# One block for three phases, K and V products sharing half of the array, and new orders of issue in a two-layer attention kernel

## The reference

```
x = x + L0_xattn(layernorm(x), ctx)   # 16 heads of 16, q from x, k and v from ctx (192 channels)
x = x + L0_ffn(layernorm(x))          # switch: 8 experts, 256 -> 1024 -> 256, 512 rows each
x = x + L1_xattn(layernorm(x), ctx)   # 16 heads of 16 with biases, then relu(. @ W1) @ W2
x = x + L1_ffn(layernorm(x))          # six nodes, each an attention of 8 heads of 32
```

## Time and profile before

| what | us |
|---|---|
| median of three runs | 4030.45 |
| profiled execution, its own time | 4034.15 |
| profiled execution, span from first to last instruction | 4032.1 |
| TensorE busy in the span | 3956.1 |
| VectorE, ScalarE, GpSimd busy | 2384.4, 2656.5, 1852.6 |
| first layer, experts, second layer end about | 624, 862, 4032 |
| from issue to landing, median: a store of an expert's rows from ScalarE's queue | 2.2 |
| from the start of `f.x2:0` (870.85) to the end of `f.rs:0` | 3.0 |

### The profile page before, as it was taken

The page is one execution under the profiler, slowest core; times in us unless marked ns, Lnnn a source line. Parts: engine busy times, 40 slices in busy tenths (PEclk is TensorE's granted clock), DMA queues, the critical chain, the costliest instruction groups (busy, mean ns, idle before and its releaser), DMA issues.

```text
span 4032.1 us, 100880 instructions
## 1 busy us (share of the span) xinstructions
PE 3956.1 (98%) x38276; PEld 3369.6 (84%) x38276; DVE 2384.4 (59%) x6216; ACT 2656.5 (66%) x11851; POOL 1852.6 (46%) x1979
## 2 busy tenths in 40 slices
...
GB/s 103 74 106 76 67 58 147 166 81 25 15 12 15 17 14 14 14 14 14 14 13 13 14 13 21 12 12 12 13 12 12 12 12 12 13 13 12 4 4 9
DMA packets 117868, 129.74 MB, mean 32 GB/s; under 512 B 12007, under 2 KB 110677, under 8 KB 117265
## 3 DMA queue, kind: packets, MB, share of 16 engines
...
...
## 4 chain that ended last, share of the span: by engine, by line
PE 76%; DVE 1%; ACT 1%; POOL 0%; issue 0%; DMA 0%; POOLq 0%; DVEq 0%
PE c_product L1552 35%; PE c_product L1563 14%; PE c_product L1614 11%; PE c_scores L1604 7%; PE c_product L1637 5%; PE c_product L1625 2%; PE c_product L1653 1%; PE c_product L1664 1%; DVE c_qT L1407 1%; PE c_product L1540 1%; PE c_product L1662 1%; ACT c_front_probs L1364 0%; ACT c_probs L1364 0%; PE c_product L1691 0%; DVE c_neg_max L1416 0%
## 5 line engine op out<-in xcount | busy, mean ns | idle before, releaser
L1318 POOL TENSOR_TENSOR c_probs<-c_probs,c_row_inv 128x512 f32<-128x512 f32 x744 | 766.5, 1042 | 1436.6 <-DVE c_row_inv L1419 1432.9
L1364 ACT ACTIVATE c_probs<-c_scores,c_neg_max 128x128 f32<-128x128 f32 x2976 | 1054.9, 398 | 432.7 <-DVE c_neg_max L1416 432.4
L1552 PE MATMUL c_product<-c_nodes,cell_w 128*128 128x256 f32 x4352 | 1049.7, 382 | 1.5 <-DVE c_nodes L1478 0.8
L1552 PEld LDWEIGHTS c_product<-c_nodes,cell_w 128*128 128x128 f32 x4352 | 794.8, 190 | 108.8 <-issue 7.3
L1416 DVE TENSOR_REDUCE c_neg_max<-c_scores 128x4 f32<-128x512 f32 x1024 | 664.7, 676 | 104.9 <-PE c_scores L1604 98.9
L1364 ACT ACTIVATION_READ_ACCUMULATOR c_probs<-c_scores,c_neg_max 128x1 f32 x2976 | 703.5, 236 | 0.0
L1370 ACT COPY c_probsT<-c_product 128x512 f32<-128x512 f32 x744 | 416.6, 616 | 235.9 <-PE c_product L1614 229.4
L1364 ACT ACTIVATE c_front_probs<-c_scores,c_neg_max 128x128 f32<-128x128 f32 x1120 | 404.6, 406 | 176.6 <-DVE c_neg_max L1416 176.4
L1563 PE MATMUL c_product<-cell_w,c_nodes 128*128 128x256 f32 x1792 | 435.3, 383 | 0.5 <-DVE c_x L1469 0.5
L474 ACT ACTIVATE a_probs<-a_scores,a_neg_max 128x128 f32<-128x128 f32 x1024 | 360.4, 410 | 47.9 <-DVE a_neg_max L545 47.6
L1614 PE MATMUL c_product<-consts_sb,c_probs 128*128 128x128 f32 x2976 | 385.8, 273 | 0.1
(11 more groups left out here) (185 smaller groups left out, 6457.8 us busy)
## 6 DMA issues: line engine op xcount, KB each, us to landing
...
```

The source lines that it names most:

```text
L1318: nc.gpsimd.tensor_tensor(e, e, rinv[:, i, r].unsqueeze(2).broadcast_to([P, 4, T]), ALU.mult).then_inc(norm_made, 1)
L1364: a = nc.scalar.activation(probs(n, j)[:, r, k], S[r][:, k], ACT.Exp, bias=nmax[:, i, r, k:k + 1], accum_out=rsum[:, i, r, k:k + 1])
L1552: i = T_.matmul(m[:, u], w[:, k, u * P:(u + 1) * P], src[:, k], start=n == 0, stop=n == last)
```

## The change

1. One `nc.Block()` is opened in `build` for all three phases. Semaphores live in a frame around it. The meeting of all engines between phases is replaced by waits: SyncE and TensorE of the experts wait until all products of the first layer are read; VectorE waits until its stores have landed; GpSimd of the second layer waits until the experts' rows have landed; TensorE's third bank of the second layer waits for VectorE's last read of the experts.
2. In the first layer a `K` that is followed directly by `V` of the job before takes the half-step form of the second layer. With the new tables that is so for job 3 and jobs 5 to 29, 26 of 32.
3. All tables of the first layer are new (repeated step, head, tail), and ScalarE gets a tail of its own there.
4. Heads and tails of the second layer are new; its repeated steps are not changed.

```
 FIRST_PE_ORDER = """
-Tn:6 Q:1 T0.1:3 T1.1:3 S0:1 A:3 r.n:7 K:0 O:3 T1.0:2 T0.0:2 S1:1 L:6 Tx:0 V:1
+K:2 V:3 Q:2 L:8 T0.1:4 T1.1:4 S0:2 A:4 Tn:7 Tx:1 r.n:8 O:4 T1.0:3 T0.0:3 S1:2
 FIRST_DVE_ORDER = """
-O^:3 S1.i3:2 st1:3 S0.i1:1 S0.i3:1 S0.i0:1 S0.i2:1 S1.x3:1 S1.x2:1 S1.x1:1 Tx^:0 L^:6 S1.x0:1 r.sh:6 V^:1
-Tn^:5 Q^:0 r.oh:6 S1.i1:1 S1.i0:1 st:-1 S0.x2:0 S0.x0:0 S0.x3:0 A^:2 r.n^:6 S1.i2:1 S0.x1:0 mk:-2 K^:-1
+S0.x3:4 S1.i2:5 A^:6 Tn^:9 r.n^:10 Tx^:3 S0.x0:4 O^:6 S0.i3:5 st1:6 S1.x1:4 S1.x3:4 S1.x0:4 S1.x2:4 S1.i1:4
+K^:3 V^:4 Q^:3 L^:9 r.sh:9 S1.i0:4 st:2 S0.i1:4 S1.i3:4 mk:2 r.oh:9 S0.i0:4 S0.i2:4 S0.x2:3 S0.x1:3
 FIRST_ACT_ORDER = """
-nm:-1 T0^1:1 S1.e3:0 S1.e2:0 S1.e1:0 r.ex:5 S1.e0:0 T0^3:1 T0^2:1 T1^3:1 T1^2:1 S0.e2:-1 S0.e3:-1 S0.e0:-1
-S0.e1:-1 T1^0:0 T1^1:0 T0^0:0
+S0.e0:4 T1^0:5 T1^1:5 T0^0:5 T0^1:5 S1.e1:4 S1.e0:4 S1.e2:4 S1.e3:4 T0^3:5 r.ex:9 T0^2:5 T1^2:5 T1^3:5 nm:2
+S0.e2:3 S0.e1:3 S0.e3:3
 FIRST_POOL_ORDER = """
-S0.n3:2 nm1:4 put:11 S0.n1:2 S1.n0:2 rs:0 S0.n2:2 S1.n1:2 S0.n0:2 S1.n2:2 S1.n3:2 rs1:3
+S0.n2:3 S0.n0:3 S1.n2:3 S0.n3:3 rs1:4 nm1:4 put:11 S1.n0:2 rs:0 S1.n1:2 S1.n3:2 S0.n1:2
...
+                    if after != ("V", j - 1):
+                        project(product(n, j), wk, ct[:, o]).then_inc(prod, 1)
+                    else:
+                        keys_m = product(n, j)
+                        for u in range(2):
+                            T_.matmul(keys_m[:, u], wk[:, 0, u * P:(u + 1) * P], ct[:, o, 0], start=u == 0, stop=False)
...
+                        for b in range(PAIR):
+                            T_.matmul(m[:, b], ct[:, o, 0, b * T:(b + 1) * T], wv[:, 0], start=b == 0, stop=False)
+                        for u in range(2):
+                            k = T_.matmul(keys_m[:, u], wk[half[0], 1, u * P:(u + 1) * P], ct[half[0], 1 - o, 1], start=False, stop=u == 1)
+                            v = T_.matmul(m[:, u], ct[half[1], o, 1, u * T:(u + 1) * T], wv[half[1], 1], start=False, stop=u == 1)
...
-        block = es.enter_context(nc.Block())
...
+            sp.wait_ge(*first["emptied"])
...
+            pe.wait_ge(*first["emptied"])
...
+            for s, n in first["stored"]:
+                dve.wait_ge(s, n)
...
+            for s, n in early["rows_of_experts"]:
+                pool.wait_ge(s, n)
...
+                elif i == BANKS // 2:
+                    pe.wait_ge(*early["experts_emptied"])
...
 PE_HEAD = """
-F6:0 F7:0 B6:0 B7:0 F8:0 f.Tx:0 f.K:0 f.V:0 f.Q:0 F9:0 f.Sb0:0 F10:0 B8:0 B9:0 B10:0 F11:0 f.Tb0.0:0 f.Tb0.1:0
+F6:0 F7:0 B6:0 F8:0 B7:0 f.Tx:0 f.K:0 f.V:0 f.Q:0 F9:0 f.Sb0:0 B8:0 F10:0 B9:0 F11:0 B10:0 f.Tb0.0:0 F12:0
...
 DVE_HEAD = """
-F6^:0 F7^:0 f.x2:0 f.st:0 F8^:0 B6^:0 B7^:0 f.x:0 f.Tx^:0 f.K^:0 f.Q^:0 f.V^:0 F9^:0 f.Sb0.x2:0 f.Sb0.x0:0
+F6^:0 F7^:0 f.x2:0 f.st:0 B6^:0 F8^:0 f.x:0 f.Tx^:0 B7^:0 f.K^:0 f.Q^:0 f.V^:0 f.Sb0.x1:0 f.Sb0.x3:0
...
+        block = es.enter_context(nc.Block())
+        phase_first_layer(nc, io, scratch, keep, cst, consts_in, cell, first, frame, block)
```

More of the change, by code:

```diff
@@ L165 @@
[L165 to L166 removed]
+rs:0 rs:1 rs:2 rs:3 S1.n3:0 S0.n0:0 S0.n2:0 S1.n1:0 S0.n1:0 S1.n2:0 S0.n3:0 S0.n2:1 S0.n1:1 S1.n0:0 S0.n0:1
+S1.n3:1 S0.n3:1 S0.n0:2 rs1:0 S1.n1:1 S0.n3:2 S1.n0:1 S1.n2:1 S0.n2:2 S0.n1:2 nm1:0 S1.n0:2 S1.n2:2 S1.n1:2
+rs:4 rs1:1 nm1:1 S1.n3:2 S0.n3:3 rs:5 S0.n1:3 S1.n0:3 S1.n1:3 S0.n2:3 S0.n0:3 rs1:2 nm1:2 S1.n2:3 S1.n3:3
@@ L178 @@
 """
 FIRST_POOL_TAIL = """
-put:8 rs1:1 nm1:1 put:7 put:6 put:5 put:4 put:3 put:2 put:1
+S0.n1:3 nm1:5 S1.n0:3 S0.n2:3 S1.n1:3 put:12 put:11 S0.n0:3 rs:1 S1.n3:3 S0.n3:3 S1.n2:3 put:10 rs1:4 S0.n3:2
+nm1:4 S0.n0:2 S0.n1:2 S0.n2:2 put:9 S1.n0:2 S0.n3:1 rs1:3 S1.n1:2 S1.n2:2 S1.n3:2 S0.n1:1 nm1:3 S0.n0:1
+S1.n2:1 S1.n0:1 S0.n2:1 S1.n1:1 S1.n3:1 put:8 put:7 rs1:2 nm1:2 put:6 rs1:1 nm1:1 put:5 put:4 put:3 put:2
+put:1
+"""
+FIRST_ACT_TAIL = """
+T0^2:4 T0^3:4 T1^2:4 T1^3:4 S0.e0:2 S0.e3:2 S0.e2:2 T1^1:3 T1^0:3 S0.e1:2 T0^0:3 nm:1 T0^1:3 S1.e1:2 S1.e0:2
@@ L185, with phase_first_layer @@
 OUT_OF_BOUNDS = 65536.0
-def phase_first_layer(nc, io, scratch, keep, cst, consts_in, cell, first):
+def phase_first_layer(nc, io, scratch, keep, cst, consts_in, cell, first, frame, block):
     x, ctx, mask, buf = io["x"], io["ctx_pairsT"], io["mask_BxS2_bf1"], scratch["buf"]
@@ L221, in phase_first_layer @@
         (FIRST_PE_HEAD, on_pe), (FIRST_DVE_HEAD, on_dve), (FIRST_ACT_HEAD, on_act), (FIRST_POOL_HEAD, on_pool)))
-    on_pe, on_dve, on_pool = (ended(tail, order, JOBS) for tail, order in (
-        (FIRST_PE_TAIL, on_pe), (FIRST_DVE_TAIL, on_dve), (FIRST_POOL_TAIL, on_pool)))
+    on_pe, on_dve, on_act, on_pool = (ended(tail, order, JOBS) for tail, order in (
+        (FIRST_PE_TAIL, on_pe), (FIRST_DVE_TAIL, on_dve), (FIRST_ACT_TAIL, on_act), (FIRST_POOL_TAIL, on_pool)))
     def is_turn(n):
@@ L321, in head_strip @@
             return int(n[1]), int(n[-1])
-        block = es.enter_context(nc.Block())
+        first["emptied"] = (prod_used, len(n_used))
+        first["stored"] = [(s, 16 * JOBS // X_RING) for s in x1_out] + [(s, 16 * JOBS // 2) for s in xn1_out]
         def halves(a):
@@ L689, in project_rows @@
                 return i
-            for n, j in on_pe:
+            keys_m = None
+            half = slice(0, P // 2), slice(P // 2, P)
+            for (n, j), after in zip(on_pe, on_pe[1:] + [None]):
                 o = j % 2
@@ L786, in _, with phase_experts @@
                     raise ValueError(n)
-def phase_experts(nc, io, scratch, cst, cell, first, early):
+def phase_experts(nc, io, scratch, cst, cell, first, early, frame, block):
     w1, w2 = io["L0_ffn_w1"], io["L0_ffn_w2"]
@@ L824, in phase_experts @@
         y_out = [sem(f"y_out{i}") for i in range(YB)]
-        block = es.enter_context(nc.Block())
+        early["rows_of_experts"] = [(s, 16 * E) for s in y_out]
+        early["experts_emptied"] = (y_made, YB * E)
         def tiles(a):
@@ L1129, with phase_second_layer @@
+e.rs:1 e.f1:1 e.f2:1
 """
-def phase_second_layer(nc, io, scratch, keep, cell, cst, early, out):
+def phase_second_layer(nc, io, scratch, keep, cell, cst, early, out, frame, block):
     ctx = io["ctx_pairsT"]
```

282 lines of the change are left out of this document (146 added, 136 removed).

## The result

The changed kernel takes **4059.66 us** (median of four runs; 4055.92 to 4062.72), the one before, beside it on the same chip, 4030.67. The ratio is 1.0074 with a 95% interval of 1.0062 to 1.0086: 0.74% slower, where 0.55% faster was forecast. The range (3991 to 4021) does not hold it.

A forecast was written before the change was run, and what follows sets the result against it. It took the first layer to be bound by four nearly full engines, the second by TensorE. Savings of 12 + 3 + 3 + 0.7 + 3 + 0.5 = 22.2 us gave 4012 profiled, median 4008, range 3991 to 4021.

The forecast's parts named there:

- The pair: First layer's K and V in half steps: 2.98 us together for 3.46, saving 0.48 us for each of 26 pairs.
- The plain step: First layer's repeated step without routing: from 16.84 to 16.5 us, a gain of 0.34.
- three limits of 16.18, 16.36 and 16.55: Plain step of the first layer, in us: ScalarE's work, TensorE's work with pairs, and the loop of x through GpSimd.
- my second rival: First layer's step does not get shorter, as ScalarE or the loop keeps it at about 16.8; 4020 us, 20%.
- The routing step: First layer's repeated step with routing: from 20.61 to 20.0 us, with ScalarE still waiting 3.5 for a maximum behind r.oh.
- The term: First layer's repeated part, plain and routing steps together: 12 us saved over 27 of 32 jobs, bounds -4 and 19.
- The head: Head of the first layer: the 3.40 us wait on V^:0 goes, 3 us saved, bounds 0 and 7.
- The tail: Tail of the first layer, all tables new: 3 us saved, with no single wait sure to go.
- The first change of phase: First layer to experts: the meeting hides behind the load, 0.7 us saved, bounds 0.3 and 0.9.
- The second change and the head of the second layer: Experts to second layer: F6 directly behind the experts, the gather earlier, 3 us saved, bounds -1 and 6.
- My rival for slower: First layer: late loads of x make the loop through GpSimd 18.2 us and the longest limit; 4048 us, 5%.

The follow-up runs named there:

- e3: The changed kernel with K and V of the first layer computed as full products again, all orders still new; 4062.46 us.
- e20: The changed kernel with r.oh in parts, its eight running sums behind O^ where GpSimd waits, A^ ahead of S0.x3, r.n ahead of S1; 4033.66 us.
- e7: The changed kernel with the eight running sums at the end of r.oh computed in six instructions, orders still new; 4050.71 us.
- e6: The changed kernel with r.oh in one piece behind the maxima and A^, r.n behind the turns, r.n^ behind O^; its measured time is not in the text.
- e1: The changed kernel with every table of before, so only the one block is new in orders; time not told from the kernel before, under 4040 us.
- e2: One block and the second layer's new heads and tails, with the first layer in its old orders; 4031.12 us.

## Why the prediction was wrong

**The pair** (2.98 us): right, 2.99, and its drains cost no more than they do in the second layer.

**The plain step** (16.84 to 16.5): wrong. It is 16.7 to 17.4, once 18.3, and no shorter in sum than before. I let three limits of 16.18, 16.36 and 16.55 meet and took hardly anything for the meeting; ScalarE works 16.31 of 16.82, and TensorE waits up to 0.72 us for it at a score round, 9.0 us in 19 such waits from 100 to 590 us. This is the mechanism of my second rival (20%), for plain steps. e3's profile adds that the pairs do shorten the new order; it starts from 17.2 to 17.8.

**The routing step** (20.61 to 20.0): this is the step of the prediction that failed. I wrote that `r.oh` "runs 4.1 us and only then takes `S0.x2`", and priced ScalarE's wait alone, "as it does now". Two things were missing. First, 4.1 us is the length of `r.oh` where GpSimd happens to stand still; in its new place it takes 5.5. Second, `r.n` and `A^` are queued behind it in the same step, so TensorE waits 1.90 and 1.96 us and then runs at the lower clock level, for which my sum had no term. ScalarE's own wait, 3.93, was close to the 3.5 forecast. I had counted who waits for the maxima and not who waits for the two instructions behind them, though the order table shows both. The term was -12 for 27 steps; measured, for the 20 from job 9 to 29, +16.3, all of it in the routing steps. e20, which changes only the places of the routing's pieces and of `A^`, has that stretch 4.2 us shorter than before. How the 4.65 us of e20's step divide into the sums' length, the place of `A^` and the rest was not separated by a run. By the windows TensorE's busy time falls by 2.73 (19.99 to 17.26) and its idle time by 1.92 (3.86 to 1.94); the rows put the clock at up to 1.76 + 1.04 = 2.8 us (`O` 3.75 for 1.99, the turns 2.98 for 1.94). That the two waits brought the lower clock is argued from their order in time.

**The head** (-3): `V^`'s wait of 3.40 is gone as forecast, but TensorE waits 11.0 us for ScalarE's exponentials up to 175 us, 2.1 before, the longest 3.45. Job 9 starts 3.0 us late; in the other profiles with this head it is 0.6 to 4.3 us, so the size is uncertain. No run tests the head alone.

**The tail** (-3, bounds -4 and 9): +10.6, of which 3.4 is one more routing step, from job 29 to 30 (23.41 against 20.04). Three `r.oh` lie in the stretch; the profile has `r.n` waiting 2.75 and 1.76 us for the sums, and e7, which shortens only them, takes 9.2 us off. But e6, which leaves the sums and the tables of the tail alone, takes 6.4 off too, so the share of the sums is open. What is left in e20, 111.5 against 107.4, I did not trace.

**The first change of phase** (-0.7): held in direction. From the issue of the load to TensorE's restart it is 4.40 us before, 4.00 in the changed kernel, 4.04 in e1 and 3.98 in e2, so 0.4 for my 0.7. The rest of e1's and e2's earlier restart lies ahead of that issue, where the kernel before has a scatter wait 3.04 us for its slots. In the changed kernel the wait for the load still ends it, at 3.83 us.

**The second change and the head of the second layer** (-3): the picture was right (F6 directly behind the experts, then TensorE idle ahead of `f.Tx`), the size was not. The gather starts 3.76 us after the experts' last product (895.28 less 891.52) where I took 2.95 (864.3 less 861.35), and lands 2.9 us after its issue where I took 2.2, so the idle time is 6.15 us, not 4. From the experts' start to the end the kernel gained 1.1 us for the forecast 3.5. e1 and e2 show no gain that their times can tell.

**My rival for slower** (the load of x, 5%) was not it: from 100 to 560 us VectorE waits 2.6 us in all for x, 11.1 before. The loss came by a way that stood among none of my rivals, and a chance of 0.04 for slower was far too low for a change that moved every instruction of four nearly full engines.

The Trainium skill, SBUF — State Buffer, section SBUF: two separate sides, says that VectorE and GpSimd share one pair of ports under an exclusive lock held for a whole instruction, taken by a VectorE instruction with two inputs in SBUF against a GpSimd one that reads SBUF. The traces agree: 0.71 to 1.12 us for two inputs and 0.18 to 0.22 for one, beside normalisations of about 1.04. It is the rule that I should have weighed.
